# Expert gates copied by DMA instead of spread by matmuls, the router one block earlier, and the new GRU state from one scan over pairs

## The reference

```
L0  s = sigmoid(x @ router_w.T + cond @ router_t_w.T); two experts of 8 by s + bias
    combine = normalised s of the chosen two, 0 for the other six
    x += (silu(x@sw1.T)*(x@sw3.T) @ sw2.T + sum_e combine_e * gelu(x@rw1_e) @ rw2_e) / 3
L1  reduces to x * gate(cond)
L2  x += a low-rank adapted two-layer MLP whose low-rank factors come from cond
L3  GRU over the 512 tokens:
    Z = sigmoid(xz + H@Whz.T + bhz);  R = sigmoid(xr + H@Whr.T + bhr)
    Ht = tanh(xh + (R*H)@Whh.T + bhh);  H = Z*H + (1-Z)*Ht
    x += H @ Whq.T + bhq
```

## Time and profile before

| | |
|---|---|
| median of 3 runs | 1326.75 us (1325.47 to 1328.45) |
| profiled execution: its time | 1327.0 us |
| profiled execution: its span | 1324.9 us, so 2.1 us lie around it |
| TensorE busy | 1278.3 us, 96% of the span |
| VectorE busy | 949.5 us, 72% |
| ScalarE busy | 389.7 us, 29% |

### The profile page before, as it was taken

How to read it: one execution, slowest core, us unless ns; L and a number is a source line. 1 busy time by engine, 2 the same in 40 slices (tenths; PEclk the granted TensorE clock), 3 DMA queues, 4 the chain that set the end, 5 groups by cost and what they waited for, 6 DMA issues and landing times.

```text
span 1324.9 us, 53882 instructions
## 1 busy us (share of the span) xinstructions
PE 1278.3 (96%) x22768; PEld 1226.7 (93%) x22768; DVE 949.5 (72%) x6173; ACT 389.7 (29%) x1734; POOL 119.8 (9%) x120
## 2 busy tenths in 40 slices
PE   6989999999999999999999999999999999999965
PEld 6389999999999999999999999999999999999864
DVE  3437777777777777777777777777777777777655
ACT  1013333333333333332333333333333332333222
POOL 2410000000000000000000000000000000000000
PEclk9999999999999999999999999999999999999855
DMA  9400000000000000000000000000000000000000
GB/s 358 136 7 3 10 11 11 11 11 10 4 10 11 11 11 11 11 7 7 11 10 11 11 11 10 7 7 11 11 11 10 11 7 7 11 10 7 7 6 6
DMA packets 8818, 27.84 MB, mean 21 GB/s; under 512 B 2920, under 2 KB 3376, under 8 KB 7296
## 3 DMA queue, kind: packets, MB, share of 16 engines
q1 hardware_dynamic: 5280, 15.41, 3.1%
q0 software_dynamic: 3296, 8.98, 2.1%
HBM read 19.94 MB, written 4.19 MB: 18 GB/s over the span
## 4 chain that ended last, share of the span: by engine, by line
PE 91%; DVE 5%; ACT 1%; DMA 1%; SPq 1%; issue 1%; POOL 0%; DVEq 0%; POOLq 0%
PE bank L363 52%; PE gate_rh L363 29%; PE gate_z L363 10%; DMA own<-in_own 1%; ACT rg L696 1%; DVE x L849 1%; DVE rhp L928 1%; DVE zm L938 0%; DVE zsum L933 0%; ACT zg L696 0%; DVE state L945 0%; DVE rh L929 0%; DVE zh L940 0%; SPq L276 0%; DVE fresh L943 0%
## 5 line engine op out<-in xcount | busy, mean ns | idle before, releaser
L363 PEld LDWEIGHTS gate_rh<-state,whp 128*128 128x128 f16 x6144 | 231.0, 97 | 27.4 <-DVE state L945 19.8
L363 PE MATMUL gate_rh<-state,whp 128*128 128x8 f16 x6144 | 235.4, 167 | 17.7 <-DVE state L945 17.7
L363 PEld LDWEIGHTS gate_rh<-rhp,whp 128*128 128x128 f16 x6144 | 230.4, 97 | 21.2 <-DVE rhp L928 15.0
L696 ACT ACTIVATE rg<-gate_rh 128x16 f32<-128x16 f32 x512 | 93.8, 183 | 519.9 <-PE gate_rh L363 519.9
L363 PE MATMUL gate_rh<-rhp,whp 128*128 128x8 f16 x6144 | 239.4, 167 | 7.5 <-DVE rhp L928 7.5
L928 DVE SCALAR_TENSOR_TENSOR rhp<-rg,hist 128x16 f16<-128x16 f32 x512 | 89.0, 174 | 180.9 <-ACT rg L696 178.7
L696 ACT ACTIVATE zg<-zsum 128x16 f32<-128x16 f32 x512 | 110.6, 216 | 227.4 <-DVE zsum L933 227.4
L363 PE MATMUL gate_z<-state,whp 128*128 128x16 f16 x4096 | 176.6, 169 | 0.0
L938 DVE TENSOR_SCALAR zm<-zg,sscale 128x16 f32<-128x16 f32 x512 | 125.7, 245 | 56.8 <-ACT zg L696 47.5
L363 PE MATMUL bank<-xt,rw 128*128 128x128 f32 x1024 | 160.2, 291 | 6.0 <-DVE sa L829 4.4
L363 PE MATMUL bank<-xt,sw 128*128 128x128 f32 x1024 | 153.4, 290 | 0.0
(11 more groups left out here) (150 smaller groups left out, 1801.8 us busy)
## 6 DMA issues: line engine op xcount, KB each, us to landing
aw<-in_aw SPq DMA_DIRECT2D x4, 2048.0 KB, 19.6
xt<-in_xT POOLq DMA_DIRECT2D x32, 128.0 KB, 2.6
out<-osb POOLq DMA_DIRECT2D x32, 128.0 KB, 2.1
rw<-in_rw SPq DMA_DIRECT2D x2, 1024.0 KB, 11.0
sw<-in_sw SPq DMA_DIRECT2D x3, 512.0 KB, 7.8
wh<-in_wh SPq DMA_DIRECT2D x3, 256.0 KB, 9.4
wx<-in_wx SPq DMA_DIRECT2D x3, 256.0 KB, 18.7
l1w<-in_l1w POOLq DMA_DIRECT2D x2, 256.0 KB, 4.3
```

The costliest lines, as they stand in the source:

```text
L363: return pe.matmul(o, w, x, start=start, stop=stop, skip_group_check=True)
L696: return act.activation(o, i, f, **kw)
```

## The change

Four things are changed.

1. `spread_gates` on TensorE is gone (8 matmuls for each block). SyncE now writes `comb` transposed to a small DRAM tensor, 1024 elements of 4 bytes, waits for `comb_out`, and reads that tensor back broadcast to all partitions into the SBUF tile `gates`, 4 KB on each. `times_gate` reads `gates`.
2. The router (scores, `add_router_bias`, `gate_op` 0 to 12) is done three blocks ahead instead of two, in other steps; the setup does the router of block 2 as well.
3. The fill stands in other steps, and the VectorE pieces of 512 columns that stand in a step's `early` are cut into two of 256.
4. The new state: ScalarE writes `ht` into every other element of `hin`, VectorE writes `zin` = (1-zg)*scale and `hin` = (1+zg)*halved, where `halved` is a new small ScalarE copy of the old state. A `tensor_tensor_scan` over the 32 elements (a running state = zin*state + hin) then gives at every second element the new state, once into `state`, once into `hist`. `zm`, `zh`, `fresh` and two `scalar_tensor_tensor` are gone.

```
+            def spread_gates(r):
+                sp.wait_ge(gating, GATE_OPS * (r + 1))
+                if r > 0:
+                    sp.wait_ge(gates_in, 16 * r)
+                sp.dma_start(gates_dram.rearrange("e t -> t e"), comb[:],
+                             allow_slow_non_contiguous=True).then_inc(comb_out, 16)
+                sp.wait_ge(comb_out, 16 * (r + 1))
...
+                sp.dma_start(gates[:].rearrange("p g c -> p (g c)"),
+                             gates_dram.rearrange("e t -> (e t)").partition_broadcast(P)).then_inc(gates_in, 16)
+
+            spread_gates(0)
             for at, i in enumerate(LOW_ORDER):
...
+            for r in range(1, BLOCKS):
+                spread_gates(r)
...
             def between_steps(m, par, s, has_y, has_l23, has_l0, has_router):
...
-                    if s == 0:
+                    if s == 1:
                         mid_base(m1)
-                    if s == 3:
+                    if s == 4:
                         up_base(m1)
...
-                if has_y and s == 1:
+                if has_y and s == 0:
                     y_out(later(m, -1), q)
...
                     if s == 11:
-                        spread_gates(m2, E47, (6, 7), cb47_done, True)
-                        pe.wait_ge(gs_done, count(m2, 1))
-                        spread_gates(m2, A3, (0, 1), cb03_done, False)
+                        l0_out(0, "s", (2, 3))
+                        l0_out(1, "s", (0,))
...
                     if s == 15:
-                        l0_out(0, "r", (2, 3))
-                        l0_out(1, "r", (0, 1, 2, 3), done=l0_done)
+                        l0_out(1, "r", (2, 3), done=l0_done)
...
             l0_whole_a((0, 1), 1)
+            pe.wait_ge(pe47_done, 2)
+            scores((0, 2), 0)
...
                     func(rg[:], rh_ps[par][:, 0, :, now], ACT.Tanh, scale=tanh_scale[R]).then_inc(rg_done, 1)
+                    bp, bs = before(par, s)
+                    act.wait_ge(st_all, n)
+                    func(halved[:], hist[:, bp, bs, :, :, 1], ACT.Copy, scale=0.5).then_inc(half_done, 1)
...
                 if k == 12:
+                    if m[1] > 0:
+                        dve.wait_ge(comb_out, 16 * m[1])
...
-                if has_y and s == 2:
+                if has_y and s == 1:
                     y_add(later(m, -1), q)
...
-                    for at, k in ((4, 1), (5, 3), (6, 4), (6, 5), (7, 7), (8, 8), (9, 9), (9, 10), (10, 12)):
+                    for at, k in ((7, 0), (8, 1), (9, 2), (10, 3), (11, 5), (12, 6), (13, 7), (15, 11), (15, 12)):
...
-                    dve.tensor_scalar(zm[:], zg[:], -1.0, sscale[:], ALU.add, ALU.mult).then_inc(zm_done, 1)
-                    dve.wait_ge(zm_done, n)
-                    dve.scalar_tensor_tensor(zh[:], zg[:], 1.0, old, ALU.add, ALU.mult)
+                    dve.tensor_scalar(zin[:, :, :, 1], zg[:], -1.0, nsscale[:], ALU.add, ALU.mult)
+                    dve.wait_ge(half_done, n)
+                    dve.scalar_tensor_tensor(hin[:, :, :, 1], zg[:], 1.0, halved[:], ALU.add, ALU.mult).then_inc(zh_done, 1)
 
                     dve.wait_ge(ht_done, n)
-                    dve.tensor_tensor(fresh[:], zm[:], ht[:], ALU.mult).then_inc(fresh_done, 1)
-                    dve.wait_ge(fresh_done, n)
-                    dve.scalar_tensor_tensor(state[:, :, 0], zh[:], 0.5, fresh[:], ALU.mult, ALU.subtract)\
+                    dve.wait_ge(zh_done, n)
+                    dve.tensor_tensor_scan(flat(state[:]), flat(zin[:]), flat(hin[:]), 0.0, ALU.mult, ALU.add)\
                        .then_inc(st_hi, 1)
-                    dve.scalar_tensor_tensor(new, zh[:], 0.5, fresh[:], ALU.mult, ALU.subtract).then_inc(st_all, 1)
+                    dve.tensor_tensor_scan(flat(new), flat(zin[:]), flat(hin[:]), 0.0, ALU.mult, ALU.add).then_inc(st_all, 1)
...
+            add_router_bias((0, 2))
+            gates_whole((0, 2))
             for i in LOW_ORDER:
                 dve.wait_ge(low_in[i], B * 16)
```

More of the change, by code:

```diff
@@ L150, in build @@
         seed = sb("seed", [P, 4, KC])
-        hist = sb("hist", [P, 2, KC, TOK])
-        state = sb("state", [P, KC, HPARTS, B], F16)
+        hist = sb("hist", [P, 2, STEPS, KC, B, 2])
+        halved = sb("halved", [P, KC, B])
+        state = sb("state", [P, KC, B, HPARTS], F16)
         rh = sb("rh", [P, KC, B])
@@ L167, in build @@
         sscale2 = sb("sscale2", [P, 1])
-        zm = sb("zm", [P, KC, B])
+        nsscale = sb("nsscale", [P, 1])
+        zin = sb("zin", [P, KC, B, 2])
+        hin = sb("hin", [P, KC, B, 2])
         rg = sb("rg", [P, KC, B])
@@ L379, in up_chunks @@
                     i.then_inc(done, 1)
-            def spread_gates(m, ps_, experts, done, last):
-                pe.wait_ge(gating, count(m, GATE_OPS))
-                for e in experts:
-                    i = mm(ps_[:, e % 4 * TOK:(e % 4 + 1) * TOK], comb[:, e:e + 1].to_broadcast([P, P]), ident[:],
-                           True, True)
-                if last:
-                    i.then_inc(done, 1)
             def l0_out(half, kind, chunks, start=False, done=None):
-                for c in chunks:
+                for n, c in enumerate(chunks):
                     w = sw2 if kind == "s" else rw2
                     g = gs[:, c * TOK:(c + 1) * TOK] if kind == "s" else ge[:, c // 4, c % 4 * TOK:(c % 4 + 1) * TOK]
-                    i = mm(l0_ps[:, half], w[:, c, half * P:(half + 1) * P], g, start and c == chunks[0], False)
+                    i = mm(l0_ps[:, half], w[:, c, half * P:(half + 1) * P], g, start and n == 0, False)
                 if done is not None:
@@ L1052, in _ @@
             dve.wait_ge(peaks_dve, 11)
-            last = hist[:, 1, :, (STEPS - 1) * B:STEPS * B]
-            dve.tensor_scalar(state[:, :, 0], condT, sscale2[:], None, ALU.mult).then_inc(st_hi, 1)
+            last = hist[:, 1, STEPS - 1, :, :, 1]
+            dve.memset(zin[:], 0.0)
+            dve.memset(hin[:], 0.0)
+            dve.tensor_scalar(nsscale[:], sscale[:], -1.0, None, ALU.mult)
+            dve.tensor_scalar(state[:, :, :, 1], condT, sscale2[:], None, ALU.mult).then_inc(st_hi, 1)
             dve.tensor_scalar(last, condT, sscale2[:], None, ALU.mult).then_inc(st_all, 1)
             dve.wait_ge(st_all, 1)
-            dve.tensor_tensor(state[:, :, 1], last, state[:, :, 0], ALU.subtract).then_inc(st_low, 1)
+            dve.tensor_tensor(state[:, :, :, 0], last, state[:, :, :, 1], ALU.subtract).then_inc(st_low, 1)
             l0_whole_b(m0)
```

224 lines of the change are left out of this document (121 added, 103 removed).

## The result

The changed kernel takes 1525.05 us (median of 4 runs, 1517.79 to 1529.96) against 1326.11 (1324.61 to 1328.45) for the kernel before: a ratio of 1.149, with a 95% interval of 1.145 to 1.154. It is 199 us slower where 20 us faster had been forecast. The profiled execution took 1526.55 us.

The account below looks back on a forecast made before the run. TensorE was taken as the bound, 96% busy, its fill setting full steps by only 0.03 us over the dependent chain. Blocks -42.3, last two blocks -2.3, setup +24.9 sum to -19.7 us: 1307 us, range 1290 to 1324.

Parts of the forecast that it names:

- hidden work: In the blocks: scores matmuls, router and both gate transfers (some 5 us) are covered by 25 us, so cost nothing.
- a clock that falls: Rival, chance 0.04: lighter steps 11 to 15 lower the granted clock, costing 3.4 us a block, about 1409 us.
- Steps 11 to 14: Each block: each loses one matmul, the chain sets 2.22 us instead of 2.31, gain 0.37 us a block.
- step 15: Last step of each block: fill from 12 records to 4, 2.40 us against 2.76, gain 0.36.
- step 0: First step of each block: y_out, needing nothing fresh, takes the place of mid_base, gain 0.24 us.
- D: Length of one scan over 32 elements on the chain, not in the trace, taken as 0.216 us.
- both scan rivals: Scan length 0.184 us, total 1296 (chance 0.2), or 0.285 us, slower than before, total 1347 (chance 0.12).
- A cheap scan: Rival, chance 0.2: scan of 0.184 us gives 1296 us; if the second wait is free as well, 1287.
- the last two blocks: After the 30 full blocks: 0.4 us from steps 0 and 2, 1.9 from 27 steps without fill, gain 2.3.
- The setup: Before the first block: the change costs 24.9 us, from block 0's gates, the clock and block 2's router.
- Block 0's gates: In the setup: write, broadcast and product stand on the path, cost 16.2 us, plus 3.4 for half clock.
- The router of block 2: In the setup, ahead of low on VectorE: cost 7.1 us, less 1.8 for removed matmuls, net 5.3.

Follow-up runs that it names:

- experiment 1: Changed kernel with comb written to DRAM as 128 rows of 32 bytes and the product reading gates with a stride; 1309.46 us, 0.986 of the kernel before.
- experiment 6: experiment 1 plus the packed, transposed 4-byte write to a DRAM tensor nobody reads, which SyncE and VectorE wait for; 1505.22 us.
- experiment 7: experiment 6 with each 4-byte element in 512, 64 or 16 bytes of DRAM of its own (three kernels); 1310.27, 1308.49 and 1312.99 us.
- experiment 9: experiment 1 plus 1024 elements of 4 bytes moved from SBUF to SBUF, each within its partition, in 8 transfers; 1309.61 us.
- experiment 2: Changed kernel with the transposed write issued twice a block, into two DRAM areas of which the first is read; 1514.1 us.
- experiment 8: experiment 6 with the added write holding one expert's gates only, 128 elements packed in 512 bytes; 1355.71 us.
- experiment 3: Kernel before the change with only the new state made by the scans; 1317.99 us, ratio 0.993.
- experiment 4: experiment 1 with the state made the old way (zm, zh, fresh) instead of by scans; 1328.42 us, ratio 1.001 to the kernel before.
- experiment 5: experiment 1 with gates of blocks 0 and 1 spread by TensorE as before and block 2's router between the setup's L2 pieces; 1281.30 us, 0.965 of the kernel before.

## Why the prediction was wrong

**The step that failed** is the one on hidden work: "The scores matmuls, the router, the transfers: hidden. [...] and the two transfers take some 5 as priced below. If that cover were gone, `ge` would come late and TensorE would stand still." The write was priced at 0.7 us, from no row, since no transfer of before writes single elements to DRAM. It takes 11 us. And the cover was never gone: `ge` does not wait for `gates` in the loop even so (write and read take 16 us, and the cover is 25). The prediction asked only who waits for the transfer's data. It did not ask what the transfer does to everything else that uses the DMA engines. Shown by the runs: the packed 4-byte write to DRAM alone makes the pause and the half clock behind it, 7.2 us a block on average over 29 blocks (experiments 1 and 6); it takes the packing (7), as many small packets do no harm by themselves (7, 9), and its length is not a sum over packets (2, 8).

The Trainium skill (DMA: Bandwidth & Descriptors, section Rules for kernel authors) says that a last dimension with a stride becomes one descriptor per element and should be laid out contiguously. The trace agrees on the count: q1 has 1040 packets in the stretch with the transposed write, and 144 in that with the rows (experiment 1, 157.24 to 158.65). This rule speaks against the change, and the prediction did not weigh it. Taken alone it would not have priced the loss: the 1024 elements at 16 bytes of distance land in 3.3 us and do no harm.

The same page of the Trainium skill (section Specifications) says that below 512 bytes the DMA engines do a read-modify-write. No run here shows one. Experiments 1 and 7 write 32 and 4 bytes at a time and are not slow, so that is not enough either. That writes to neighbouring bytes wait for each other would fit the dependence on distance, but no experiment tells it from other reasons, and the 7.5 us of experiment 8 are not explained by it. Why packing makes the write slow stays open.

**How the write stops the recurrence** stays open. The traces show that packets of other queues take longer meanwhile (GpSimd's 0.64 us instead of 0.12), instruction packets among them: in blocks 1 to 29 those of q8 that start within 10 us of a write's issue take 2.2 us on average and up to 6.8, the others 1.1. In each of the 29 blocks the longest step is step 1 or 2. The reading that suggests itself is that an engine runs out of fetched instructions. Three things speak against it.

- In these blocks TensorE, VectorE and ScalarE are idle together 33 times for more than 0.8 us. In 13 of the 33 no instruction packet is under way from the start of the pause to its end. One of them ends at 962.18 (ScalarE, and the queues from 953.7 to 962.2):

```profile
962.18 0.18 ACT L711 ACTIVATE hin<-gate_rh 128x16 f32<-128x16 f32 x1 [4.32 <-remote]
```

```profile
q0 software_dynamic: 71, 0.21, 27.9%
q1 hardware_dynamic: 1040, 0.00, 5.5%
```

No instruction packet stands there, nor from 962.2 to 966; ScalarE goes on without one.
- In 30 of the 33 ScalarE is the first to go on, and in the pause shown with the result TensorE has done its fill before it stops. But q8 goes with TensorE: 22255 + 22256 rows on 174 packets here and 22768 + 22768 on 178 before are 256 rows a packet both times. That it carries TensorE's instructions is an estimate from this.
- In experiment 8 the q8 packets behind a write are slowed as much (2.6 us on average), and yet there are 8 such pauses, 13 us in all, where the changed kernel has 33 and 94 us.

So what ScalarE waits for is not shown.

**What a block pays.** Against experiment 1 the 29 blocks from block 1 on cost 1272.93 / 29 = 43.9, instead of (1102.07 - 36.5) / 29 = 36.7. TensorE is idle for 123.4 us of those blocks, 4.3 a block, where experiment 1 has 0.3; and it is busy for 1149.5 us, where experiment 1 has about 1058, which is 3.1 a block for the half clock. The rival "a clock that falls" (0.04) named the second half, with the wrong trigger: the lighter steps don't bring the clock down (1.00 in the blocks of experiments 1, 3, 4 and 5); it falls behind a pause.

**The terms that held**, by block 0 and by experiment 1:
- Steps 11 to 14. These are `rg` starts of block 0 after the change, steps 11, 12 and 15 and the first step of block 1:

```profile
157.97 0.18 ACT L711 ACTIVATE rg<-gate_rh 128x16 f32<-128x16 f32 x1 [1.09 <-PE gate_rh L388]
160.15 0.18 ACT L711 ACTIVATE rg<-gate_rh 128x16 f32<-128x16 f32 x1 [0.47 <-PE gate_rh L388]
...
166.69 0.18 ACT L711 ACTIVATE rg<-gate_rh 128x16 f32<-128x16 f32 x1 [0.96 <-PE gate_rh L388]
169.07 0.18 ACT L711 ACTIVATE rg<-gate_rh 128x16 f32<-128x16 f32 x1 [1.16 <-PE gate_rh L388]
```

160.15 - 157.97 is 2.18 us, and (166.69 - 157.97) / 4 as well, forecast 2.22; step 15 takes 2.38, forecast 2.40. A block of experiment 1 takes 36.74, forecast 38.15 - 1.41 = 36.74. That it agrees to the hundredth is luck: by the `rg` starts of blocks 1 to 29, steps 11 to 14 give 0.5 us instead of 0.37, and step 0 gives 0.12 instead of 0.24.
- The scan. The group rows of after:

```profile
L976 DVE TENSOR_TENSOR_SCAN state<-zin,hin 128x32 f16<-128x32 f32 x512 | 115.0, 225 | 161.1 <-ACT hin L711 107.5
...
L978 DVE TENSOR_TENSOR_SCAN hist<-zin,hin 128x32 f32<-128x32 f32 x512 | 102.0, 199 | 0.8 <-issue 0.8
```

D was taken as 0.216 and is 0.225 into fp16 and 0.199 into fp32. The bound from the reduce, 0.184, was too low and the one from `scaled`, 0.285, too high; so the lengths of both scan rivals fall. But one half of *A cheap scan* came true: the second wait, priced at 0.05, is free. In the rows of the step above `hin` starts at 659.89 and the scan at 660.11, 0.22 us later, which is what `ht` and `fresh` took before. That is why the steps set by the chain come out at 2.18 and not 2.22.
- Without the transposed write the whole comes out at 1309.46 us, 2.5 above the forecast of 1307.
- From the last two blocks 2.3 us had been expected. The kernel after gives 2.3 and experiment 5 gives 2.2 (1281.0 - 1198.17 = 82.8), but experiment 1 nothing (1309.0 - 1224.03 = 85.0, as before). The first 9 us of block 30 tell them apart, in experiment 1 and in experiment 5:

```profile
1224.03:1233.00 8.97, 7.90 (x115) 7.32 (x112) 4.96 (x31) 3.05 (x14) 0.69 (x1) 0.62 0.06 16
```

```profile
1198.17:1207.14 8.97, 7.28 (x155) 6.66 (x151) 6.29 (x40) 4.01 (x19) 0.69 (x1) 1.00 0.06 16
```

In experiment 1 the granted clock is down from the start of block 30, in experiment 5 only later. Why it falls sooner there is not shown, and nor is whether it does so in each of its runs. It is in these rows that the gain goes.

**The setup** was forecast at +24.9 us and measured +37.2.
- Block 0's gates. This is the timeline of after:

```profile
37.92 0.59 SPq L283 DMA_DIRECT2D gates_t<-comb  x1
53.19 0.33 SPq L289 DMA_DIRECT2D gates<-gates_t  x1
57.86 1.29 DVE L867 TENSOR_TENSOR ge<-pe_e,gates 128x512 f32<-128x512 f32 x2 [23.08 <-DMA gates<-gates_t]
...
58.61 6.62 PE L388 MATMUL bank<-ge,rw 128*128 128x128 f32 x32 [24.53 <-DVE ge L867]
...
110.68 0.33 SPq L289 DMA_DIRECT2D gates<-gates_t  x1
110.77 0.23 DVE L843 SCALAR_TENSOR_TENSOR comb<-chosen,den,scaled 128x8 f32<-128x8 f32 x1 [4.38 <-DMA gates_t<-comb]
```

The write was to land at 48.0 and lands at 53.2 (48.4 in experiment 1, as forecast). The read takes 4.7, not 3.7. The 32 matmuls take 6.62 us, not 3.74, at a granted clock of 0.56: 2.9 more, where 3.4 were foreseen. TensorE ends at 65.2, forecast 56.1 + 3.4 = 59.5. So this part costs 65.23 - 39.88 = 25.4 us instead of 19.6.
- The router of block 2. A wait was overlooked: `comb` must not be written again before the second write has landed, and 4.38 us go to it; `low` stands behind it, at 111.00. The rest of the setup costs 37.2 - 25.4 = 11.8 us with this wait, and 5.3 had been forecast; some 2 us are not taken apart.
- With rows the setup costs 121.96 - 95.35 = 26.6 us, near the 24.9. Experiment 5 shows that all of it belongs to the two things it puts back, the transfers of the first gates and the place of block 2's router: without them the setup costs 0.3 us more than before.

## What to carry to other kernels

For a transfer that nobody waits for, ask also what shares the DMA engines with it. Look at how its bytes fall in DRAM: a 4 KB write in rows of 32 bytes lands in 1.4 us, and the same 4 KB scattered as 4-byte elements side by side takes 11 and halts the recurrence for some microseconds. Turn the data on the side of the reader: here the product with a stride takes 0.62 us instead of 0.42 for 256 columns, four times a block, and the blocks take what was forecast even so. And a loop gain is worth measuring without its setup: with the gates in rows this change brings 1.4%, and 3.5% once the first two blocks keep their old gates and block 2's router has a better place.

## What the runs showed of the hardware that had not been expected

- Time to land of small writes to DRAM in this kernel, from issue to the issue of what waits for it: 128 x 32 bytes 1.4 us; 1024 x 4 bytes packed 11.2 to 11.7; the same twice into two areas 11.25. By SyncE's mean wait, with the 32-byte write ahead of it: 1024 x 4 bytes packed 10.3; each in 512, 64 or 16 bytes of its own 2.6, 2.7 and 3.3; 128 x 4 bytes packed 7.5. Why twice as much takes no longer, and an eighth nearly three quarters of it, stays open.
- During a packed write the packets of GpSimd's queue took 0.64 us instead of 0.12, and those of the instruction queue q8 up to 6.8 instead of 1.1.
- After TensorE had been idle for 3 us in the loop (657.4 to 660.4) the granted clock was 0.56 over 661.0 to 668.0, although TensorE was busy for all of them.
- A scan over 32 elements takes 0.225 us with an fp16 result and 0.199 with an fp32 one, next to 0.184 for a reduce that reads as many.
- A VectorE product of 256 columns takes 0.42 us with both operands in order and 0.62 when one of them is read with a stride of 8 elements (the changed kernel and experiment 1).
